# Attention front re-ordered: x in halves, rows of four heads sent out first, second batch split by ScalarE and GpSimd, first turn of the maxima earlier and on two queues

## Chip, cores and metric

One core of a Trainium2 chip runs the whole program. The metric is device time of one execution in microseconds (us); lower is better. Engines: TensorE (PE), VectorE (DVE), ScalarE (ACT), GpSimd (POOL), and SyncE (SP), which only issues transfers here. "SPq" and "ACTq" in the rows are transfers issued by SP and ACT.

## What is computed

Two layers of a small network on x of 2 batches x 1024 tokens x 128 channels. Only the first block matters for the change:

```python
mod = (silu(L0_c) @ L0_wmod)          # sa, ca, ga, sb, cb, gb: six rows of 128 for each batch
h = layernorm(x) * (1 + ca) + sa
q, k, v = h @ Wq.T, h @ Wk.T, h @ Wv.T     # 16 heads of 8 channels
attn = softmax(q @ k.T / sqrt(8))          # 1024 x 1024 for each of 2 x 16 heads
x = x + ga * (attn @ v)
```

Behind it follow a coupling network, two Mamba blocks and a mixture of 8 experts, which the change doesn't touch.

## The kernel before

Everything is written out by hand: each engine has its own instruction stream, in program order, and semaphores tie them together (`wait_ge`, `then_inc`). An engine whose next instruction waits does nothing else.

**Exact products from bfloat16.** The products q.k need float32 precision, so every q and k value is split into three bfloat16 parts: `hi` = the value rounded, `mid` = the rounded rest, `lo` = the rest of the rest. `pe_project` (L774) makes a float32 chunk of q or k (128 rows, which are 16 heads x 8, by 512 tokens) in a PSUM bank. ACT copies it to bfloat16 (`ac_part_hi`, L780), DVE subtracts (`part_rest`, L787) and, for the first batch, casts to `mid` (L791). For the second batch ACT casts (`ac_part_mid`, L796). GpSimd makes `lo` (L801). A side (0 = q, 1 = k) and a chunk c (0, 1 = first batch, 2, 3 = second) name a tile; `project(c)` does both sides.

**Way through DRAM.** SP writes the parts to the DRAM tensor `qk_parts` (`sp_parts_out`, L804, six transfers of 128 partitions for a batch, 256 KB each). They come back stacked in 48 rows for a head (`q_rows`, `k_rows`), so that one bfloat16 matmul of 48 rows sums all part products. The first group is heads 0 to 3: `load_first` (L518) brings heads 0 and 2 (12 transfers of 8 rows, on SP and ACT), `sp_load(0, 1)` heads 1 and 3. GpSimd's `po_ones` (L476) sets rows of ones in `k_rows`.

**Maxima ahead.** The softmax needs each query's maximum before its exponentials. The 32 heads are done in 16 legs (`NLEG`) of 4 heads x 512 queries. A leg has 16 tiles of maxima: two matmuls into `max_ps` (L559, `pe_max_score`) and one DVE reduction of 128x1024 (L570, `ve_max_score`); two such tiles fit in PSUM, so the matmuls of tile t wait for the reduction of tile t-2. `AHEAD` = 22 tiles are done before the main loop, by `ahead(v)` for v = 0 to 21. When a leg's 16 tiles are done, GpSimd splits the maxima (L579 to L585), PE turns them (`pe_max_turn`, L601), ACT copies the turned rows (L607), and SP writes them under the `q_rows` in four transfers (`sp_max_turn`, L610), so that the second pass of scores (L678) comes out with the maximum taken off. The main loop (L932) then weaves maxima (m), scores and exponentials (s, ACT, L686) and products with v (v, L706); its first item is one half of maxima tile 22, its second is the first score.

**Order of the front, before.** Layer norm of the first batch: 8 statistics, 8 `bn_aggr`, one GpSimd root of 128x8 (`ln_root`, L362), 8 `ve_ln_apply` (L358). Then transposes (`turn`, L398; L409 on PE, L416 on ACT), `project(0)`, `project(1)`, `values` (v, L814), parts out, the rows of layer 0's modulation (`mod_row`, L296, a matmul and an ACT copy each), the loads of the first group, layer norm and transposes of the second batch, the rows and columns of layer 1's modulation, and only then `ahead(0)`, `project(2)`, `ahead(1)`, `ahead(2)`, `project(3)`, `values(2)`, `values(3)`, parts out, `ahead(3)` to `ahead(21)`. The turn of leg 0 stands in `ahead(18)`:

```python
if v == NU + 2:
    ...
    max_turn(0)
    for half in range(2):
        sp_load(1, half)
```

The four PSUM banks of `score_k` are handed round as a ring (`ring.take`): `turn`, `pe_project`, `values`, `mod_row` and `pe_mod_cols` each take the next bank and wait until ACT or DVE has read what was in it.

## Time and profile before

| | us |
|---|---|
| median of 3 runs | 1132.33 (1130.43 to 1132.64) |
| the profiled execution's own time | 1135.81 |
| its span | 1134.5 |
| first tile of maxima starts on PE | 30.73 |
| first score of the main loop on PE | 60.94 |

Busy shares over the span: PE 92%, DVE 85%, ACT 72%, GpSimd 46%. Those are means over stages with different limits; the change lies in the first 61 us. The times in the rows are us from the span's start, save where ns is said. A float32 matmul appears as two records, and the ends of matmuls are modelled; starts are to be trusted more. "idle before" names how long the engine had nothing and what released it.

### The profile page before, as it was taken

Reading aid. Unit: us, or ns where it says so; the run is one execution under the profiler, and the core shown is the slowest. Engines: PE = TensorE matmul, PEld = TensorE weight load, DVE = VectorE, ACT = ScalarE, POOL = GpSimd, SP = SyncE. Lnnn points to the kernel's source line nnn. Section 1 sums busy time; section 2 is a strip of 40 time slices with the busy share of each in tenths; the row PEclk is TensorE's granted clock in tenths of the full one; section 3 lists DMA queues with packets and bytes.
Section 4 is the critical chain, followed back from the end, with each engine's and each line's share of the span. In section 5 each row is a group of like instructions: output and inputs, shape, how many; then the busy total and the mean of one; then the engine's idle time right before and its main releaser. Section 6 shows DMA issues by size and latency. Waiting matters only on the chain. (4 is left out here: it accounts for less than half of the span.)

```text
span 1134.5 us, 21410 instructions
## 1 busy us (share of the span) xinstructions
PE 1043.9 (92%) x7835; PEld 650.8 (57%) x7835; DVE 969.5 (85%) x1327; ACT 818.4 (72%) x1593; POOL 517.9 (46%) x487
## 2 busy tenths in 40 slices
PE   6899999999999887989999999899999996599997
PEld 4222222222222333458988984468888984388896
DVE  6899999999995676979999996989999999866666
ACT  3279898999999544978888854888888833246652
POOL 5400441010101111027889982048999974146663
PEclk9779999999999888799999999899999997699999
DMA  5210100001004420107999980118999977512224
GB/s 158 71 44 15 30 16 17 29 16 31 16 2 76 131 57 2 59 1 191 241 249 226 221 210 3 59 28 191 232 246 230 229 184 259 131 50 64 62 64 126
DMA packets 60313, 121.04 MB, mean 107 GB/s; under 512 B 15471, under 2 KB 28783, under 8 KB 59953
## 3 DMA queue, kind: packets, MB, share of 16 engines
q0 software_dynamic: 15440, 52.66, 23.2%
q1 hardware_dynamic: 43064, 64.82, 18.6%
q10 hardware_dynamic: 1704, 2.20, 0.6%
q8 instruction: 63, 1.03, 0.4%
q14 instruction: 42, 0.34, 0.1%
HBM read 58.02 MB, written 13.19 MB: 63 GB/s over the span
## 5 line engine op out<-in xcount | busy, mean ns | idle before, releaser
L2267 PEld LDWEIGHTS m_pair<-filter_w,delta_x_t 128*128 128x128 f32 x2560 | 294.0, 192 | 43.3 <-issue 43.3
L2267 PE MATMUL m_pair<-filter_w,delta_x_t 128*128 128x112 f32 (+3 forms) x2560 | 298.7, 276 | 9.4 <-DVE h_t L2294 4.1
L570 DVE TENSOR_REDUCE neg_max<-max_ps 128x1 f32<-128x1024 f32 x256 | 293.5, 1214 | 10.8 <-PE max_ps L559 10.5
L686 ACT ACTIVATE exp_scores<-score_k 128x512 f32<-128x512 f32 x512 | 273.9, 599 | 20.7 <-PE score_k L678 13.4
L2243 ACT ACTIVATE decay<-delta,a_log 128x1024 f32<-128x1024 f32 x128 | 145.7, 1142 | 50.0 <-DVE normed L2294 28.7
L559 PE MATMUL max_ps<-k_rows,q_rows 48*128 48x512 bf16 x512 | 166.8, 404 | 7.7 <-DVE neg_max L570 6.5
L2235 ACT ACTIVATE filter_w<-filter,b_t 128x112 f32<-128x112 f32 (+1 forms) x576 | 167.4, 374 | 0.0
L706 PE MATMUL score_k<-exp_scores,v_cols 128*32 128x256 f32 x2048 | 165.1, 396 | 0.0
L678 PE MATMUL score_k<-q_rows,k_rows 51*128 51x512 bf16 x512 | 162.8, 391 | 0.6 <-DMA q_rows<-neg_max_rows 0.6
L579 POOL CAST neg_max_parts<-neg_max 128x16 bf16<-128x16 f32 x16 | 3.1, 196 | 228.8 <-DVE neg_max L570 228.8
L559 PEld LDWEIGHTS max_ps<-k_rows,q_rows 48*128 48x128 bf16 x512 | 30.1, 95 | 120.6 <-DVE neg_max L570 91.9
L706 PEld LDWEIGHTS score_k<-exp_scores,v_cols 128*32 128x32 f32 x2048 | 40.9, 108 | 98.9 <-ACT exp_scores L686 80.1
L2285 DVE TENSOR_TENSOR_SCAN m_pair<-decay,m_pair 128x1024 f32<-128x1024 f32 x38 | 87.0, 2290 | 1.6 <-PE m_pair L2267 1.2
L2332 POOL TENSOR_TENSOR h_t<-h_t,c_row 128x1024 f32<-128x1024 f32 x30 | 81.5, 2717 | 13.1 <-DVE h_t L2294 13.1
L2332 POOL TENSOR_TENSOR normed<-normed,c_row 128x1024 f32<-128x1024 f32 x28 | 75.8, 2706 | 24.1 <-DVE normed L2294 24.1
L2294 DVE TENSOR_TENSOR_SCAN normed<-decay,m_pair 128x1024 f32<-128x1024 f32 x32 | 73.0, 2281 | 8.7 <-PE m_pair L2267 8.7
L2294 DVE TENSOR_TENSOR_SCAN h_t<-decay,m_pair 128x1024 f32<-128x1024 f32 x32 | 73.0, 2281 | 6.0 <-PE m_pair L2267 6.0
L2380 PE MATMUL m_pair<-delta_x,ident 128*128 128x512 f32 x136 | 68.3, 598 | 0.0
L2962 ACT ACTIVATE silu_gate<-gate 128x512 f32<-128x512 f32 x39 | 24.5, 628 | 55.4 <-DVE gate L2957 50.9
L2989 POOL DMA_INDIRECT moe_out_rows<-tile_out,row_to x37 | 39.8, 1075 | 42.1 <-DVE tile_out L2983 34.7
L2919 POOL DMA_INDIRECT tile_rows<-moe_normed,row_from x39 | 37.9, 972 | 37.5 <-DVE row_to L2794 25.9
L2935 ACT ACTIVATE gate_up<-gate_up_all 128x1024 f32 x39 | 41.1, 1056 | 17.8 <-DVE row_empty L2792 17.1
(343 smaller groups left out, 1726.9 us busy)
## 6 DMA issues: line engine op xcount, KB each, us to landing
c_row<-c_rows SPq DMA_DIRECT2D x64, 512.0 KB, 6.3
x_inner<-normed POOLq DMA_DIRECT2D x16, 512.0 KB, 6.7
delta_x<-mod_memory POOLq DMA_DIRECT2D x15, 512.0 KB, 8.0
delta_x<-x_inner POOLq DMA_DIRECT2D x15, 512.0 KB, 9.0
x_inner<-h_t POOLq DMA_DIRECT2D x14, 512.0 KB, 6.5
mod_memory<-h_t POOLq DMA_DIRECT2D x14, 512.0 KB, 9.1
mod_memory<-normed POOLq DMA_DIRECT2D x12, 512.0 KB, 9.3
gate_up_all<-in_gate_up_w SPq DMA_DIRECT2D x8, 512.0 KB, 7.5
```

Of the source, the lines that this page charges most:

```text
L559: mm = pe.matmul(mps[:, t % 2 * 2 + half, :], qp[row:row + KR, s, leg % 2, qt * P:(qt + 1) * P], kp[row:row + KR, s, half * CH:(half + 1) ...
L570: ve.tensor_reduce(nm[leg % 2][:, 4 * j + qt:4 * j + qt + 1], mps[:, bank:bank + 2, :].rearrange("p a q -> p (a q)"), AX_X, ALU.max, negat ...
L678: pe.matmul(eps[:, bank, :], kp[row:row + KM, s, kt * P:(kt + 1) * P], qp[row:row + KM, s, leg % 2, :], start=True, stop=True).then_inc(*s ...
L686: ac.activation(pt[a % 4][:, HEADS[r % 4], :], eps[:, bank, :], ACT.Exp, scale=SC).then_inc(*exped.up())
L706: mm = pe.matmul(eps[32 * j:32 * j + 32, av_bank[leg], qs], va[quad % 2][:, j, kt, :], pt[a % 4][:, j, qs], start=(kt == half == 0), stop= ...
L2235: w = ac.activation(wf[g % 3][:, lo:c * STEP + P], tri[min(c, 1)][:], ACT.Copy, scale=self.bT[b][:, c, n:n + 1])
L2243: ac.activation(da[u % 4], delta[:, blk, b, :], ACT.Exp, scale=am[:, l, blk, n:n + 1]).then_inc(*decay.up())
L2267: mm = pe.matmul(vps[blk][:, lo:hi], self.duT[b][:, c, blk * P:(blk + 1) * P], wf[g % 3][:, lo:hi], start=True, stop=True)
L2285: ve.tensor_tensor_scan(to, da[u % 4], vps[0][:], 0.0, ALU.mult, ALU.add).then_inc(*hs.up())
L2294: ve.tensor_tensor_scan(hh[g % 4], da[u % 4], vps[1][:], 0.0, ALU.mult, ALU.add).then_inc(*hs.up())
L2332: po.tensor_tensor(yacc[b][1] if n == 1 else hh[g % 4], hh[g % 4], csb[g % 3][:], ALU.mult).then_inc(*yg.up())
L2380: pe.matmul(yps[:, c * CH:(c + 1) * CH], self.ident[:], yp[k][:, c * CH:(c + 1) * CH], start=False, stop=last, skip_group_check=True).then ...
```

## The change

- x of the first batch comes in two transfers of four tiles each, and each half has statistics, aggregation and a root of its own; x of the second batch is issued behind six weight transfers. The load of layer 1's modulation moves on ACT's queue behind `silu` and `identb`. `silu` of layer 1 and its spread move behind the first group's loads. `ve_mod_cols(0)` moves behind the first batch's `ve_ln_apply`.
- The first batch's four tiles: `mid` is cast by DVE for tile 0 alone and by ACT for the other three; `lo` is GpSimd's for tiles 0 to 2 and DVE's for tile 3.
- The parts of heads 0 to 3 (32 of 128 partitions) go out first; those of heads 4 to 15 are issued behind the first group's loads. In `load_first`, ACT issues q's `hi` alone (3 transfers); SP issues the other nine.
- `po_ones(2, NS)` moves ahead of the second batch's work on GpSimd.
- The second batch: ACT makes `hi` and also copies the float32 values to SBUF, GpSimd subtracts (`rest`), ACT casts `mid`, GpSimd makes `lo`. DVE has no part in it. One tile stands behind each of `ahead(0)` to `ahead(3)`, `values` behind `ahead(4)` and `ahead(5)`, a `mod_row` of layer 1 behind each of `ahead(6)` to `ahead(9)`, the matmuls of its columns behind `ahead(10)` and their reading behind `ahead(12)`. Both transposed chunks of the second batch are read by ACT.
- The turn of leg 0 moves from `ahead(18)` to `ahead(17)`, its four transfers are issued two by SP and two by ACT, and the second batch's parts go out behind `ahead(21)`, so behind the 18 transfers of `sp_load(1, ...)`.

```diff
-            def sp_max_turn(leg):
-                sp.wait_ge(turn_read.sem, leg + 1)
-                for j in range(4):
-                    s, row = head_rows(leg, j)
-                    sp.dma_start(qp[row + KR:row + KM, s, leg % 2, :].rearrange("a (k q) -> a k q", k=4),
-                                 mt[leg % 2][12 * j:12 * j + 12, :]).then_inc(*max_in[leg % 2].up(16))
+            def put_max_turn(leg):
+                for engine, heads in ((sp, (1, 0)), (ac, (3, 2))) if leg == 0 else ((sp, range(4)),):
+                    engine.wait_ge(turn_read.sem, leg + 1)
+                    for j in heads:
+                        ...
...
+            self.ac_load_modulation(1)
+            half = TB // 2
+            roots = [self.ln_root(self.X, i * half, (i + 1) * half, [self.in_x[i].at()]) for i in range(2)]
+            self.po_spread(0)
+            normed = [self.ve_ln_apply(self.X, t, roots[t // half]) for t in range(TB)]
+            self.ve_mod_cols(0, cols_ps)
+            scaled = self.m_scale
+            root = self.ln_root(self.X, TB, NT, [self.in_x[2].at()])
...
-                if v == NU + 2:
+                if v == NU + 1:
                     for m in ring.out():
                         pe.wait_ge(*m)
+                    pe.wait_ge(*self.identb_set.at())
                     max_turn(0)
+                    for part in range(3):
+                        sp.wait_ge(*to_dram[0][part].at())
+                    sp.wait_ge(*rows_set.at())
                     for half in range(2):
                         sp_load(1, half)
...
+                def first_batch_parts():
+                    tiles, rest_in = [(c, side) for c in range(2) for side in range(2)], []
+                    for n, tile in enumerate(tiles):
+                        bank = ring.take()
+                        pe_project(*tile, bank)
+                        ac_part_hi(*tile, bank)
+                        rest_in.append(ve_part_rest(*tile, bank))
+                        if n == 0:
+                            po_part_lo(*tile, ve_part_mid(*tile, rest_in[0]))
+                        if n > 1:
+                            po_part_lo(*tiles[n - 1], ac_part_mid(*tiles[n - 1], rest_in[n - 1]))
+                    ve_part_lo(*tiles[3], ac_part_mid(*tiles[3], rest_in[3]))
...
+                def second_batch_parts(c, side):
+                    bank = ring.take()
+                    pe_project(c, side, bank)
+                    ac_part_hi(c, side, bank)
+                    ac_part_copy(c, side, bank)
+                    rest_in = po_part_rest(c, side, bank)
+                    if rest_known:
+                        second_batch_mid()
+                    rest_known.append(((c, side), rest_in))
...
-                for c in range(2):
-                    project(c)
+                first_batch_parts()
                 for c in range(2):
                     values(c)
-                sp_parts_out(0)
-                rows_in[0] = [self.mod_row(0, j) for j in range(4)]
+                sp_parts_out(0, range(4), ((part_hi.at(),), (part_mid.at(), part_ve.at()), (part_po.at(), part_ve.at())))
                 for engine in (sp, ac):
                     engine.wait_ge(*early_rows)
+                first_q = qp[:].rearrange("d s a q -> d s (a q)")
                 for part in range(3):
                     load_first(sp, kp, 1, part)
-                    load_first(ac if part < 2 else sp, qp[:].rearrange("d s a q -> d s (a q)"), 0, part)
+                    load_first(sp if part else ac, first_q, 0, part)
                 sp_load(0, 1)
-                po.wait_ge(*part_lo.at())
+                sp_parts_out(0, range(4, H), ((), (), ()))
+                self.ac_silu_c(1)
+                rows_in[0] = [self.mod_row(0, j) for j in range(4)]
+                self.po_spread(1)
                 po_value_columns()
+                po_ones(2, NS)
                 ve.wait_ge(*self.ln_aggr.at())
                 normed += [self.ve_ln_apply(self.X, t, root) for t in range(TB, NT)]
-                self.turn(normed, col(1), col(0), (scaled,), done=ht, by=(0, 0, 0, 1), chunks=(2, 3))
-                rows_in[1] = [self.mod_row(1, j) for j in range(4)]
-                self.ve_mod_cols(1, self.pe_mod_cols(1))
-                ahead(0)
-                project(2)
-                ahead(1)
-                ahead(2)
-                project(3)
-                for c in range(2, NC):
-                    values(c)
-                sp_parts_out(1)
-                po.wait_ge(*part_lo.at())
-                po_ones(2, NS)
-                sp.wait_ge(*rows_set.at())
+                self.turn(normed, col(1), col(0), (scaled,), done=ht, by=(0, 0, 0, 0), chunks=(2, 3))
+                for v in range(AHEAD):
+                    ahead(v)
+                    if v < 4:
+                        second_batch_parts(2 + v // 2, v % 2)
+                    elif v < 6:
+                        if rest_known:
+                            second_batch_mid()
+                        values(v - 2)
+                    elif v < 10:
+                        rows_in[1].append(self.mod_row(1, v - 6))
+                    elif v == 10:
+                        cols_ps = self.pe_mod_cols(1)
+                    elif v == 12:
+                        self.ve_mod_cols(1, cols_ps)
+                sp_parts_out(1, range(H), ((part_hi.at(),), (part_mid.at(),), (part_po.at(),)))
...
-            pe.wait_ge(*self.identb_set.at())
-            for v in range(3, AHEAD):
-                ahead(v)
```

## Rows read from the trace of the kernel before

**Rows 1.** Page, part 5, the two costliest groups of the attention loop.

```profile
L570 DVE TENSOR_REDUCE neg_max<-max_ps 128x1 f32<-128x1024 f32 x256 | 293.5, 1214 | 10.8 <-PE max_ps L559 10.5
L686 ACT ACTIVATE exp_scores<-score_k 128x512 f32<-128x512 f32 x512 | 273.9, 599 | 20.7 <-PE score_k L678 13.4
```

**Rows 2.** Windows: each engine's busy time (instructions), granted clock, DMA share, GB/s.

```profile
23.50:24.00 0.50, 0.00 (x0) 0.00 (x0) 0.50 (x2) 0.00 (x0) 0.50 (x1) 1.00 0.95 295
25.00:25.50 0.50, 0.50 (x4) 0.38 (x3) 0.25 (x1) 0.00 (x0) 0.00 (x0) 0.50 0.88 295
28.00:28.50 0.50, 0.50 (x2) 0.24 (x2) 0.00 (x0) 0.32 (x2) 0.00 (x0) 0.93 0.23 78
...
81.00:102.00 21.00, 21.00 (x225) 5.82 (x223) 20.53 (x20) 20.26 (x40) 1.95 (x9) 1.00 0.11 33
```

**Rows 3.** Timeline of DVE, 0 to 70 us: start, length, what.

```profile
5.07 1.65 DVE L346 BATCH_NORM_STATS2 bn_parts<-x 128x6 f32<-128x128 f32 x8 [5.07 <-DMA x<-in_L_attn_x]
...
15.21 0.69 DVE L787 TENSOR_TENSOR part_rest<-score_k,part 128x512 f32<-128x512 f32 x1 [0.93 <-ACT part L782]
15.94 0.43 DVE L791 CAST part<-part_rest 128x512 bf16<-128x512 f32 x1
...
17.00 0.88 DVE L791 CAST part<-part_rest 128x512 bf16<-128x512 f32 x1
...
20.84 4.42 DVE L358 TENSOR_SCALAR normed<-x,mean_var,rstd 128x128 f32<-128x128 f32 x8
...
31.37 1.23 DVE L570 TENSOR_REDUCE neg_max<-max_ps 128x1 f32<-128x1024 f32 x1
...
38.48 22.40 DVE L570 TENSOR_REDUCE neg_max<-max_ps 128x1 f32<-128x1024 f32 x19 [0.42 <-PE max_ps L559]
```

**Rows 4.** Timeline of PE, 0 to 70 us.

```profile
12.50 4.62 PE L777 MATMUL score_k<-h_t,w_qkv 128*128 128x512 f32 x8
16.95 1.95 PE L814 MATMUL score_k<-w_qkv,h_t 128*128 128x128 f32 x16
...
24.22 1.56 PE L409 MATMUL score_k<-ident,normed 128*128 128x128 f32 x6 [1.57 <-DVE normed L358]
...
29.40 1.40 PE L256 MATMUL score_k<-silu_c,mod_memory 128*128 128x2 f32 x12
30.73 0.60 PE L559 MATMUL max_ps<-k_rows,q_rows 48*128 48x512 bf16 x2
31.26 1.98 PE L777 MATMUL score_k<-h_t,w_qkv 128*128 128x512 f32 x4
...
56.00 0.30 PE L601 MATMUL score_k<-identb,neg_max_parts 128*48 128x128 bf16 x1
...
60.94 0.61 PE L678 MATMUL score_k<-q_rows,k_rows 51*128 51x512 bf16 x1 [0.59 <-DMA q_rows<-neg_max_rows]
```

**Rows 5.** Timeline of GpSimd, 0 to 70 us.

```profile
22.24 1.85 POOL L750 MEMSET v_cols<- 128x1024 f32 x2
...
38.20 2.27 POOL L801 TENSOR_TENSOR part<-part_rest,part 128x512 bf16<-128x512 f32 x2 [1.39 <-ACT part L796]
40.52 7.06 POOL L478 MEMSET k_rows<- 32x4096 bf16 x2
```

**Rows 6.** Groups by shape: busy us, mean ns | idle before.

```profile
L342 POOL TENSOR_TENSOR rstd<-var_eps,minus_half 128x4 f32<-128x4 f32 x2 | 2.0, 1010 | 0.2
```

**Rows 7.** Timeline of ACT, 0 to 70 us.

```profile
14.58 0.60 ACT L782 ACTIVATE part<-score_k 128x512 bf16<-128x512 f32 x1 [1.12 <-PE score_k L777]
...
56.34 0.27 ACT L607 ACTIVATE neg_max_rows<-score_k 48x128 bf16<-48x128 bf16 x1 [16.27 <-PE score_k L601]
```

**Rows 8.** Timeline of SP: the transfers that it issues.

```profile
17.78 0.58 SPq L808 DMA_DIRECT2D qk_parts<-part  x1
...
27.59 0.31 SPq L523 DMA_DIRECT2D q_rows<-qk_parts  x1
...
56.68 3.15 SPq L614 DMA_DIRECT2D q_rows<-neg_max_rows  x4
```

**Rows 9.** The issues of `sp_parts_out` (L808) by line: time to landing.

```profile
DMA to landing us min/median/max: 2.8/2.9/4.3
```

More of the change, by code:

```diff
@@ L193, in constants @@
         self.gtmp = {n: sb(f"gate_tmp{n}", [P, 2 * n]) for n in (NB, NB * D)}
-        self.in_x = [self.sig(f"in_x{b}") for b in range(NB)]
+        self.in_x = [self.sig(n) for n in ("in_x_first", "in_x_next", "in_x_second_batch")]
         self.in_c = [self.sig(f"in_c{l}") for l in range(2)]
@@ L207, in constants @@
         self.ac_load_modulation(0)
-        for b in range(NB):
-            sp.dma_start(self.X[:, b * TB:(b + 1) * TB, :],
-                         A["L0_attn_x"][b].rearrange("(k p) d -> p k d", p=P)).then_inc(*self.in_x[b].up(16))
-            if b == 0:
-                sp.dma_start(self.ident[:], A["k_ident"]).then_inc(*self.in_k.up(16))
+        for half in range(2):
+            lo = half * TB // 2
+            sp.dma_start(self.X[:, lo:lo + TB // 2, :], A["L0_attn_x"][0][lo * P:(lo + TB // 2) * P].rearrange(
+                "(k p) d -> p k d", p=P)).then_inc(*self.in_x[half].up(16))
+        sp.dma_start(self.ident[:], A["k_ident"]).then_inc(*self.in_k.up(16))
         po.memset(self.half[:], -0.5).then_inc(*self.const_set.up())
@@ L782, in ac_part_hi, with ve_part_rest @@
                     ac.activation(p[0][:, side, c * CH:(c + 1) * CH], bank.ps[:], ACT.Copy).then_inc(*part_hi.up())
-                def ve_part_mid(c, side, bank):
+                def ve_part_rest(c, side, bank):
                     cs = slice(c * CH, (c + 1) * CH)
@@ L825, in ac_values, with second_batch_mid @@
                     return bank.left
-                def project(c):
-                    banks = [ring.take() for _ in range(2)]
-                    for side in range(2):
-                        pe_project(c, side, banks[side])
-                        ac_part_hi(c, side, banks[side])
-                        ve_part_mid(c, side, banks[side])
-                        if c < 2:
-                            po_part_lo(c, side)
-                    if c > 1:
-                        for side in range(2):
-                            ac_part_mid(c, side, banks[side].left)
-                            po_part_lo(c, side)
+                def first_batch_parts():
[10 more added lines that the diff above has]
+                    ve_part_lo(*tiles[3], ac_part_mid(*tiles[3], rest_in[3]))
+                rest_known = []
+                def second_batch_mid():
+                    tile, rest_in = rest_known.pop()
+                    po_part_lo(*tile, ac_part_mid(*tile, rest_in))
+                def second_batch_parts(c, side):
[7 more added lines that the diff above has]
+                    rest_known.append(((c, side), rest_in))
                 def values(c):
```

77 lines of the change are left out of this document (45 added, 32 removed).

## The prediction

> **What bounds the kernel now.** I read the page first, then the timelines of the five engines from 0 to 70 us, then windows of half a microsecond for the clock. In the attention loop all three large engines are nearly full: in 21 us PE shows 21.00, DVE 20.53, ACT 20.26 [rows 2]; its costliest groups, 256 reductions and 512 exponentials, hardly idle [rows 1]. The change alters nothing there, for the same 22 tiles are ahead. So what counts is when the first score starts, 60.94 us [rows 4], and everything behind it should move with it.
>
> What sets 60.94? Go backwards. The score waited 0.59 us for the turned maxima's rows [rows 4]. Their four transfers were issued from 56.68 for 3.15 us [rows 8], behind ACT's copy at 56.34 [rows 7] and the turn at 56.00 [rows 4]. Had they been in, the score would still have stood behind the first half of maxima tile 22, which waits for the reduction of tile 20. The reductions are a stream: tile 0 starts at 31.37, the last 19 run without a gap from 38.48 to 60.88, 1.18 us each [rows 3]. 22 of them need 25.9 us; the stream took 60.88 - 31.37 = 29.5. The missing 3.6 us are the second batch's four subtractions, 4 x 0.69 = 2.8, and gaps of 0.8 around them [rows 3]. And why does tile 0 start so late? PE came to its matmuls at 30.73, straight from layer 1's columns (29.40, 1.40 us long), so PE's order had the last word there [rows 4]. The data weren't much earlier: SP's last issue for the first heads was at 27.59 [rows 8], and landing takes some 1.7 us, which I estimate from the turned rows (last of four issues begun near 59.1, score released at 60.94 [rows 4, 8]). That gives 29.3.
>
> **The change, part by part.** I follow the new order with these durations.
>
> *Layer norm.* x lands at 5.07 as a whole [rows 3]; its first half can't take longer, and I take 4.2. Four statistics (0.21 each) and four aggregates lead to a root of 1.01 for 4 columns [rows 3, 6], so both halves are normalized by about 9.3. But the scale comes from PE's columns, whose inputs the change hardly hastens, so I let the first projection start near 11.3, against 12.50 [rows 4].
>
> *First batch's parts.* The first projection took 2.08 us from start to ACT (12.50 to 14.58 [rows 4, 7]), PE being slow there; two at full speed took 1.98 with their modelled end [rows 4], 0.86 apart. So `hi` of the four tiles is ready at 17.3 (ACT now has a cast in between), against 17.78, when SP saw it before [rows 8]. The casts and `lo` end at 19.4: one DVE cast less per tile removes 0.43 to 0.88 each [rows 3], and DVE does the last `lo` (0.69, priced as the subtraction L787) beside GpSimd's 1.14 [rows 5]. Before, SP could issue `lo` at about 22.3, since 6 issues of about 0.6 end where its loads begin.
>
> The row shows a DVE cast of 0.43 alone and 0.88 beside GpSimd's `lo`, and eight normalizations of 4.42 in all while GpSimd set `v_cols` from 22.24 [rows 3, 5]. The Trainium skill ("SBUF — State Buffer", Who interferes with whom) says that such a DVE instruction and a GpSimd one exclude each other for a whole instruction, and that a DVE instruction with two SBUF inputs waits for a GpSimd one that reads. By that rule DVE's last `lo` would wait for GpSimd's, 0.5 us later than I have it; by it, too, reductions never wait for GpSimd. The trace agrees on the latter: the 19 reductions keep 1.18 beside 7.06 us of GpSimd's fills [rows 3, 5].
>
> *Out and back.* SP issues `hi` at 17.3, `mid` at 19.4 (its mark is DVE's count after the last `lo`), `lo` at 20.5. Unknown is what a transfer of 32 partitions costs: an issue between 0.31 (8 rows) and 0.58 (128 rows) [rows 8], landing between 2.8 and 4.3 [rows 9]. I take 0.55 and 2.9, the short end, for a quarter of the bytes. `lo` is in at 23.9. SP's nine loads (2 more than before) take about 0.4 each and the last is issued near 25.0, in at 26.8. With landing 4.3 it is 28.2; with everything short, 25.3. ACT's q loads and the layer 0 rows are done by 25, the second batch's transposes by 26, so PE waits for the data: **tile 0 at 26.8 instead of 30.73, 3.9 sooner**. The normalizations have 1 to 2 us of cover there; if GpSimd's fills of 3.5 us each (half of 7.06 [rows 5]) caught one, it would be gone.
>
> *The stream of maxima.* From a first reduction at 27.4, 22 x 1.175 = 25.9 us would end at 53.3. DVE gets `ve_mod_cols(1)`, 0.45. The four subtractions are gone from it (ACT 0.60 each for the copy, GpSimd about 1.2 each, nearest `lo` 1.14 [rows 5]; 1.4 at most would add 1 us to its chain). But PE now has work between the tiles. At full clock: 12 pairs x 0.43, four projections x 0.86, two `values` (1.95 for two [rows 4]), four rows (2 x 0.86 + 2 x 0.43), columns 1.40: 14.6 us until tile 11. The clock will not be full all the time. Before, PE was empty for 1.57 us until 24.22 [rows 4], and the granted clock was 0.50 by 25.0, 0.93 at 28.0 again [rows 2]; after, PE is sparse from 20 to 26.8. I charge 4 us at half speed, so 2 us: 16.6. DVE alone would reach tile 11 after 11 x 1.175 + 0.6 = 13.5. The difference, **3.1 us, is stalls of DVE behind PE**.
>
> *Behind them the banks.* GpSimd's `po_ones` (7.06) and `v_cols` (1.85 and two short ones) [rows 5] now precede its subtractions. They start when ACT has done layer 1's `silu`, about 22.2, and end near 31.8. ACT's `mid` of the first tile waits for the first subtraction (33.0), and behind it in ACT's order stand `hi` and copy of tile 2, and so on; ACT frees `values(2)`'s bank near 40.3, `mod_row`'s third take needs it, and PE comes there at 39.4. This adds 0.9. `max_turn(0)`'s copy comes near 51, 9 us after ACT's last of these, so it isn't touched. Nor are the second batch's parts: leg 4 is their first user.
>
> *The turn.* One tile earlier and two queues: PE comes to the turn 1.18 earlier than the 56.00 of before, 1.0 after tile 15's reduction (60.88 - 6 x 1.18 = 53.8), about when GpSimd's split is done; with 0.6 for turn and copy [rows 4, 7] and the hand-over the copy ends 1.75 after that reduction, two issues on each side take 3.15 / 2 = 1.6 [rows 8], landing 1.8: 5.1 after tile 15. PE reaches the score after tile 20's reduction (5 x 1.175 = 5.9) and 0.43 for the first half of tile 22. The wait is gone and the score starts 0.7 before the last reduction ahead ends, where before it started with its end: 0.7 to 0.8 won. ACT's two issues lie before a table load and the first exponential; both fit in.
>
> **Sum.** Last reduction ahead: 27.4 + 25.9 + 0.45 + 3.1 + 0.8 = 57.6. First score 56.9, against 60.94: **4.0 us sooner**. In terms: start -3.9, subtractions and gaps -3.6, columns +0.45, stalls +3.1, banks +0.8, turn -0.75. The profiled execution took 1135.81, so it would be 1131.8; the median of the runs is 3.5 below it: 1132.33 - 4.0 = **1128.3 us**. The loop's start at half clock stays as it was: PE is again sparse for over 10 us before it.
>
> **Rivals.**
> - *Transfers are better than priced and PE's clock holds.* Tile 0 at 25.3 (1.5 more), the 2 us at half speed and part of the bank wait fall away, too: 6.5 won, 1125.8. For it: a quarter of the bytes. Against: PE's idle stretch. Chance 0.19.
> - *Transfers are the bound and don't shrink.* Landing 4.3 for each part and nine issues on one queue: tile 0 at 28.5 to 29, about 2 won, 1130.3. For it: before, `lo` needed the long landing. Chance 0.19, split by the 0.2% bound.
> - *A start gained and lost again later*: the loop's start moves against the clock's dips, or ACT and PE run slower through the first exponentials. Loss 2 to 4 us, 1131 to 1133, no change. Against: loads and weights further back have no absolute due time. Chance 0.11.
> - *Slower: the clock stays at half through the interleaving.* PE's 14.6 us become about 29, less what DVE hides; tile 11's matmuls end near 56 instead of 44, and the score starts 8 us later than before: 1140. It decides from stalls of 3.1 + 4.8 = 7.9 us, that is, from roughly 8 us at half clock instead of 4. For it: a projection behind each pair doubles PE's need just when its clock is low. Against: in the same front, the clock was back 4 us after dense work began at 24.22 [rows 2, 4]. Chance 0.08.
>
> My forecast gets 0.43. 0.2% is 2.3 us, about what a measurement of this kernel tells from no change; the bound is 1130.07. Faster: 0.43, 0.19, and half of the second rival, 0.09, together 0.71. Same: 0.10 of the second and 0.10 of the third, 0.20. Slower: 0.08 and 0.01 of the third, 0.09. The range reaches from the first rival with a microsecond more to the third: 1124.3 to 1132.3; it leaves out the fourth and the far ends.
>
> **What would show it.** `part` out at 17.3 and again for the other heads behind the loads; the first `max_ps` matmul at 26.8 with a DMA as its releaser; no `part_rest` on DVE beyond 20; DVE gaps with PE as releaser among the first 12 reductions, 3 to 4 us in all; the first score near 56.9 with no wait on a DMA. A first tile later than 29, or gaps above 8 us, makes the prediction wrong; so does a score on time with an end that isn't.

## The result and the profile after

| | before | after |
|---|---|---|
| median of six runs each, us | 1132.34 (1130.43 to 1135.05) | 1148.11 (1146.29 to 1152.20) |
| profiled execution: own time / span, us | 1135.81 / 1134.5 | 1149.29 / 1148.0 |
| mean granted clock of TensorE | 0.941 | 0.931 |

The change is slower: the ratio is 1.0144, with an interval from 1.0121 to 1.0167. I had predicted 1128.3 and put 1140 at a chance of 0.08. The medians differ by 15.8 us, the two profiled executions by 13.5; the account below is that of the profiled ones.

The page of the kernel after, the group of the reductions. It answers to the first of [rows 1]: the reductions take as long as before, but DVE stands idle in front of them, behind PE, for 36.4 us instead of 10.5.

```profile
L571 DVE TENSOR_REDUCE neg_max<-max_ps 128x1 f32<-128x1024 f32 x256 | 294.1, 1211 | 36.5 <-PE max_ps L560 36.4
```

The timeline of DVE after:

```profile
18.73 1.00 DVE L826 TENSOR_TENSOR part<-part_rest,part 128x512 bf16<-128x512 f32 x1 [0.70 <-ACT part L814]
...
28.89 1.22 DVE L571 TENSOR_REDUCE neg_max<-max_ps 128x1 f32<-128x1024 f32 x1 [7.11 <-PE max_ps L560]
31.85 1.22 DVE L571 TENSOR_REDUCE neg_max<-max_ps 128x1 f32<-128x1024 f32 x1 [1.74 <-PE max_ps L560]
...
60.46 2.35 DVE L571 TENSOR_REDUCE neg_max<-max_ps 128x1 f32<-128x1024 f32 x2 [2.39 <-PE max_ps L560]
...
69.19 5.93 DVE L571 TENSOR_REDUCE neg_max<-max_ps 128x1 f32<-128x1024 f32 x5 [0.20 <-PE max_ps L560]
```

This is where the time went. The stream of maxima starts earlier (28.89 against 31.37 in [rows 3]), and then its first eleven tiles take 60.46 - 28.89 = 31.6 us where DVE alone needs 11 x 1.175 = 12.9: **18.6 us of stalls**, 1.74 between most neighbours, all with a PE matmul as releaser. PE's own timeline says why:

```profile
11.43 5.09 PE L780 MATMUL score_k<-h_t,w_qkv 128*128 128x512 f32 x8 [0.78 <-ACT h_t L418]
...
23.28 1.07 PE L411 MATMUL score_k<-ident,normed 128*128 128x128 f32 x8 [2.25 <-issue]
27.82 1.03 PE L560 MATMUL max_ps<-k_rows,q_rows 48*128 48x512 bf16 x2 [3.47 <-DMA q_rows<-qk_parts]
28.78 2.07 PE L780 MATMUL score_k<-h_t,w_qkv 128*128 128x512 f32 x2
30.79 1.03 PE L560 MATMUL max_ps<-k_rows,q_rows 48*128 48x512 bf16 x2
...
72.82 0.60 PE L680 MATMUL score_k<-q_rows,k_rows 51*128 51x512 bf16 x1
```

A pair of maxima takes 1.03 with its modelled end, against 0.60 in [rows 4]. There is no gap between the entries from 27.82 on: PE works all the time, slowly. The windows show the clock (columns: us, length, busy us of PE, weight loads, DVE, ACT, GpSimd with instructions, granted clock, DMA share, GB/s):

```profile
20.00:22.00 2.00, 1.03 (x4) 0.38 (x2) 1.78 (x7) 0.04 (x1) 0.00 (x0) 1.00 0.18 57
...
24.00:26.00 2.00, 0.35 (x4) 0.11 (x2) 0.00 (x0) 1.55 (x3) 1.89 (x5) 0.63 0.37 115
26.00:28.00 2.00, 0.18 (x1) 0.12 (x2) 0.00 (x0) 0.00 (x0) 2.00 (x1) 0.50 0.45 124
...
27.50:61.00 33.50, 33.18 (x70) 12.00 (x70) 14.00 (x12) 9.97 (x24) 13.82 (x10) 0.50 0.15 46
...
73.00:86.00 13.00, 12.44 (x68) 1.86 (x64) 10.49 (x9) 8.69 (x16) 0.00 (x0) 0.50 0.52 165
86.00:107.00 21.00, 21.00 (x225) 5.84 (x221) 20.16 (x18) 20.14 (x39) 0.83 (x4) 1.00 0.07 20
```

The clock falls from 1.00 to 0.50 (from 2.4 to 1.2 GHz) near 24.5: the 0.63 is the mean of 24 to 26. PE's wait for the first rows has then only just begun; ahead of it lie the transposes of 1.07 us and a standstill of 2.25. The clock stays at half for over 60 us, although PE is busy for 33.18 us of the 33.50 from 27.5 to 61. It is back at 86. So the first score starts at 72.82, against 60.94, and the loop's first 13 us run at half clock.

The kernel before loses the clock at the same time, as its windows show (stretches that [rows 2] hasn't), but is back at 28, behind transposes and rows of layer 1. What it has and the kernel after hasn't is the rise, not a clock that never falls. Its loop runs at half clock for 8 us:

```profile
24.50:25.00 0.50, 0.50 (x4) 0.35 (x2) 0.50 (x3) 0.00 (x0) 0.00 (x0) 0.65 0.94 295
...
61.00:69.00 8.00, 7.62 (x39) 1.29 (x39) 6.61 (x6) 6.31 (x12) 0.00 (x0) 0.50 0.32 97
```

ACT's first exponential comes 11.9 us later than before, its copy at the end of the loop's first leg 14.35 later (99.55 against 85.20), the copy of the last leg 14.05 later (383.66 against 369.61), the end of the span 13.5 later. From the first leg's copy to the last's both kernels take nearly the same time, 284.4 us before and 284.1 after, with 18.77 us for most legs. So the loss arises ahead of 100 us.

The following three views serve the account of the single terms below. SP's timeline:

```profile
17.33 5.03 SPq L835 DMA_DIRECT2D qk_parts<-part  x6
...
25.91 0.30 SPq L524 DMA_DIRECT2D q_rows<-qk_parts  x1
...
68.52 1.54 SPq L616 DMA_DIRECT2D q_rows<-neg_max_rows  x2
```

Time to landing of the issues of L835, all 18 of them (before: [rows 9]):

```profile
DMA to landing us min/median/max: 2.9/3.4/3.9
```

ACT's timeline:

```profile
68.22 0.27 ACT L608 ACTIVATE neg_max_rows<-score_k 48x128 bf16<-48x128 bf16 x1 [11.96 <-PE score_k L602]
68.52 1.63 ACTq L616 DMA_DIRECT2D q_rows<-neg_max_rows  x2
...
73.47 1.73 ACT L688 ACTIVATE exp_scores<-score_k 128x512 f32<-128x512 f32 x3 [2.00 <-PE score_k L680]
```

### The profile page after: what moved, and what is told of

The parts are those of the page before. It is cut to its first block and busy times, and to the rows that moved or that the text cites. A ratio compares the mean times of both kernels' runs of the same rounds, so it can differ in the third digit from the quotient of the medians.

```text
span 1148.0 us, 21428 instructions
## 1 busy us (share of the span) xinstructions
PE 1054.6 (92%) x7835; PEld 655.2 (57%) x7835; DVE 966.8 (84%) x1320; ACT 821.5 (72%) x1601; POOL 522.4 (46%) x492
## 3 DMA queue, kind: packets, MB, share of 16 engines
q8 instruction: 63, 1.03, 0.4%
## 5 line engine op out<-in xcount | busy, mean ns | idle before, releaser
L571 DVE TENSOR_REDUCE neg_max<-max_ps 128x1 f32<-128x1024 f32 x256 | 294.1, 1211 | 36.5 <-PE max_ps L560 36.4
L560 PE MATMUL max_ps<-k_rows,q_rows 48*128 48x512 bf16 x512 | 170.3, 411 | 9.2 <-DVE neg_max L571 5.2
L2377 POOL TENSOR_TENSOR normed<-normed,c_row 128x1024 f32<-128x1024 f32 x28 | 76.4, 2727 | 23.7 <-DVE normed L2339 23.7
L2377 POOL TENSOR_TENSOR h_t<-h_t,c_row 128x1024 f32<-128x1024 f32 x30 | 81.4, 2714 | 11.9 <-DVE h_t L2339 11.8
L3007 ACT ACTIVATE silu_gate<-gate 128x512 f32<-128x512 f32 x39 | 24.5, 628 | 55.7 <-DVE gate L3002 44.7
L2980 ACT ACTIVATE gate_up<-gate_up_all 128x1024 f32 x39 | 41.1, 1056 | 17.9 <-DVE row_empty L2837 17.1
```

Of the source, the lines that this page charges most:

```text
L560: mm = pe.matmul(mps[:, t % 2 * 2 + half, :], qp[row:row + KR, s, leg % 2, qt * P:(qt + 1) * P], kp[row:row + KR, s, half * CH:(half + 1) ...
L571: ve.tensor_reduce(nm[leg % 2][:, 4 * j + qt:4 * j + qt + 1], mps[:, bank:bank + 2, :].rearrange("p a q -> p (a q)"), AX_X, ALU.max, negat ...
L2377: po.tensor_tensor(yacc[b][1] if n == 1 else hh[g % 4], hh[g % 4], csb[g % 3][:], ALU.mult).then_inc(*yg.up())
```

## The experiments

Theory A: PE's wait in front of tile 0 lets the clock fall, and the work that is woven between the tiles doesn't bring it back. Rivals: the woven order itself costs this much at any clock (B); GpSimd's and ACT's longer chain for the second batch holds the banks (C); the transfers or their small pieces (D). Every kernel computes the full result; the matmuls that some of them add are extra work whose result nobody reads. The times are medians, each beside that of the kernel before on the same chip; since those differ (1118 to 1132), only ratios are compared between chips. A ratio with an interval is the recorded estimate, which needn't be the quotient of the two medians; a kernel that ran once has no interval. What is said of clocks and of times within the kernel comes from one trace of each.

### Fill PE's wait, with full rows and with fewer (e1_fill, e2_fill48)

```diff
+                def pe_fill(n, rows=P):
+                    for _ in range(n):
+                        pe.matmul(mps[:, 3, :], w[0:rows, 0, :], self.HT[0:rows, 0:CH], start=True, stop=True)
...
                 rows_in[0] = [self.mod_row(0, j) for j in range(4)]
+                pe_fill(2)
...
                 self.turn(normed, col(1), col(0), (scaled,), done=ht, by=(0, 0, 0, 0), chunks=(2, 3))
+                pe_fill(4)
                 for v in range(AHEAD):
```

The second kernel has `pe_fill(2, 48)` and `pe_fill(4, 48)`: the same matmuls with 48 of the 128 rows.

> The changed kernel with six float32 matmuls of 128 rows x 512 columns added on TensorE, whose results nobody reads: two behind the rows of layer 0 and four between the transposes of the second batch and the first tile of maxima, where TensorE was idle. Theory A (the clock: TensorE's idle stretch before the first tile lets the granted clock fall to half, and the woven work between the tiles then runs at half): the clock stays 1.00 through the interleaving, tiles 0 to 10 come 1.5 to 2 us apart instead of 3.0, the first score starts at 56 to 59 us instead of 72.8, and the time is 1128 to 1133. Rival B (weaving other matmuls between the tiles costs this much at any clock): first score still beyond 68 us, time 1144 or more. Rival C (the clock is low for another reason than idleness, such as the kind of work): clock 0.50 again by 35 us, time over 1142.

> As the fill with 128 rows, but the six added matmuls use 48 of the 128 rows, for the same time. If any busy time holds the clock, this gives the same as the full fill: clock 1.00, 1128 to 1133. If the number of rows in use counts, the clock falls as without a fill: 0.50 from about 26 us on, first score near 73, time near 1148.

With full rows 1118.96 against 1118.81, ratio 1.0006 (0.9990 to 1.0022). Its windows and DVE's timeline:

```profile
24.00:28.00 4.00, 3.89 (x16) 2.27 (x16) 0.00 (x0) 2.60 (x6) 3.88 (x6) 1.00 0.37 117
...
32.00:46.00 14.00, 14.00 (x59) 5.99 (x58) 11.38 (x10) 8.53 (x22) 10.32 (x9) 1.00 0.26 85
```

```profile
31.32 1.23 DVE L571 TENSOR_REDUCE neg_max<-max_ps 128x1 f32<-128x1024 f32 x1 [0.37 <-PE max_ps L560]
...
46.80 2.36 DVE L571 TENSOR_REDUCE neg_max<-max_ps 128x1 f32<-128x1024 f32 x2 [0.74 <-PE max_ps L560]
```

With 48 rows a single run gave 1133.46, ratio 1.013, as slow as the change. Its windows and PE's timeline:

```profile
24.00:28.00 4.00, 4.00 (x15) 1.88 (x13) 0.00 (x0) 1.90 (x4) 3.88 (x5) 1.00 0.40 127
28.00:32.00 4.00, 4.00 (x8) 1.11 (x8) 1.58 (x2) 1.09 (x2) 3.94 (x2) 0.61 0.37 111
32.00:46.00 14.00, 14.00 (x32) 5.23 (x31) 5.77 (x5) 6.63 (x17) 9.73 (x9) 0.50 0.22 74
```

```profile
28.17 0.59 PE L560 MATMUL max_ps<-k_rows,q_rows 48*128 48x512 bf16 x2
28.69 1.96 PE L780 MATMUL score_k<-h_t,w_qkv 128*128 128x512 f32 x2
30.58 1.03 PE L560 MATMUL max_ps<-k_rows,q_rows 48*128 48x512 bf16 x2
```

The first run takes the whole loss away with nothing but filler, so the clock is the cause, and B, C and D can at most hold the rest. The second is finer than theory A: there PE never waits (4.00 of 4.00 from 24 to 32), the pair of tile 0 still runs at the full clock, and within a microsecond the clock goes down. In this run a busy PE wasn't enough; what it worked on counted. And the woven order, the same in both, keeps the full clock where it meets it (1.00 from 32 to 46) and the half where it meets that. Two groups from tile 0 to tile 12 (windows from 28 to 61 and from 29 to 47), first the kernel after, then e1_fill (busy us, mean ns | idle):

```profile
L560 PE MATMUL max_ps<-k_rows,q_rows 48*128 48x512 bf16 x26 | 13.2, 619 | 3.5 <-DMA q_rows<-qk_parts 3.5
L780 PE MATMUL score_k<-h_t,w_qkv 128*128 128x512 f32 x8 | 8.3, 1141 | 0.0
```

```profile
L560 PE MATMUL max_ps<-k_rows,q_rows 48*128 48x512 bf16 x26 | 7.7, 381 | 0.3 <-DMA q_rows<-qk_parts 0.3
L780 PE MATMUL score_k<-h_t,w_qkv 128*128 128x512 f32 x8 | 4.5, 644 | 0.0
```

The same instructions in the same number take 13.2 instead of 7.7 us and 8.3 instead of 4.5. And even at the full clock the first eleven tiles take 46.80 - 29.73 = 17.1 us, 4.1 more than DVE alone: a pair and one woven item (a projection or a part of the values) are 1.59, and DVE's reduction of 1.23 is done 0.37 earlier.

### Layer 1's rows and columns ahead of the tiles again (e3_rows_first), and the woven order alone (e4_before_spread)

```diff
                 self.turn(normed, col(1), col(0), (scaled,), done=ht, by=(0, 0, 0, 0), chunks=(2, 3))
+                rows_in[1] = [self.mod_row(1, j) for j in range(4)]
+                self.ve_mod_cols(1, self.pe_mod_cols(1))
                 for v in range(AHEAD):
...
-                    elif v < 10:
-                        rows_in[1].append(self.mod_row(1, v - 6))
-                    elif v == 10:
-                        cols_ps = self.pe_mod_cols(1)
-                    elif v == 12:
-                        self.ve_mod_cols(1, cols_ps)
```

The other kernel is the one before, with these lines moved the other way, and projections and values one behind each tile; ACT and DVE split as before.

> The changed kernel with the rows and columns of layer 1's modulation back in front of the first tile of maxima, where they stood before the change. They fill TensorE's idle stretch with work that has to be done. Theory A: the first tile starts 1 to 2 us later (29 to 30 us), but the clock is 1.00 by 30 us, 4 to 5 us of work are gone from between the tiles, first score 56 to 60 us, time 1128 to 1134. Rival B: only the removed work is saved, at half clock 9.9 us of it less 2 us of later start: first score near 65, time near 1140. Rival C: as B.

> The kernel before with only its order behind the transposes changed as in the changed kernel: one tile of the second batch behind each of the first four tiles of maxima, then values, rows and columns one by one; all else (transfers, VectorE's subtractions, the turn) as before. Theory A: TensorE reaches the first tile from sparse work, waits for data, the clock is half and stays there; first score at 68 to 74 us, time 1140 to 1148: the loss comes from this part alone. If it comes from other parts (ScalarE's copy, GpSimd's subtractions, transfers), the time is within 3 us of 1132.

e3: 1117.82 against 1118.81, ratio 0.9992 (0.9978 to 1.0007). e4, one run: 1134.94, ratio 1.014. Windows of e3, and its timelines of DVE and ACT:

```profile
24.00:28.00 4.00, 3.78 (x20) 2.75 (x20) 0.00 (x0) 3.79 (x10) 3.88 (x6) 1.00 0.38 115
...
46.00:60.00 14.00, 12.05 (x32) 1.66 (x31) 13.80 (x13) 3.68 (x6) 1.54 (x8) 0.50 0.15 43
58.00:70.00 12.00, 11.44 (x64) 1.86 (x64) 9.74 (x9) 8.52 (x16) 0.00 (x0) 0.50 0.57 173
```

```profile
39.33 14.02 DVE L571 TENSOR_REDUCE neg_max<-max_ps 128x1 f32<-128x1024 f32 x12 [0.40 <-PE max_ps L560]
```

```profile
57.83 4.57 ACT L688 ACTIVATE exp_scores<-score_k 128x512 f32<-128x512 f32 x8 [2.00 <-PE score_k L680]
```

And e4's PE:

```profile
29.75 1.03 PE L559 MATMUL max_ps<-k_rows,q_rows 48*128 48x512 bf16 x2 [4.06 <-DMA q_rows<-qk_parts]
30.72 2.07 PE L777 MATMUL score_k<-h_t,w_qkv 128*128 128x512 f32 x2
32.72 1.03 PE L559 MATMUL max_ps<-k_rows,q_rows 48*128 48x512 bf16 x2
```

In e4 nothing else of the change is in, and the whole loss is there: a wait of 4.06 us, tiles 2.97 apart, first exponential at 76.4. In e3 all else is in, and the loss is gone. So one part of the change did it: the 5 us of layer 1's rows and columns used to fill the wait for the transfers, with matmuls on all 128 rows, and were moved behind it. In e3 PE also stands for 2.22 us in front of the transposes, as in the change, but dense work follows from 24.22 to tile 0 and the clock stays at 1.00.

e3 is nearly the front that I had predicted: first exponential at 57.8 instead of 61.6, 3.8 sooner. But the end doesn't show it. At the end of the first leg 1.3 us of it are left (83.94 against 85.20), at the last leg 1.7 (367.93 against 369.61). The windows say where it went: the clock, which fell at 44 when only tiles of 48 rows were left for PE, stays at half until 70, for 13 us of the loop instead of 8.

### Keep the clock up behind tile 6 (e5_warm, e6_before_warm, e9_warm192, e10_warm256)

```diff
+                def pe_warm(rows=P, cols=384):
+                    pe.wait_ge(ring.free[7], ring.used[7])
+                    pe.matmul(eps[:, 3, 0:cols], w[0:rows, 0, :], self.HT[0:rows, 0:cols], start=True, stop=True)
...
                         values(v - 2)
+                    if v >= 6:
+                        pe_warm()
```

This stands on e3 (384, 192 and 256 columns), and for e6 on the kernel before, behind each of the tiles 3 to 21.

> The kernel with the rows and columns of layer 1 in front, and one float32 matmul of 128 rows x 384 columns added behind each of the tiles of maxima 6 to 21, whose result nobody reads. The kernel without them started its exponentials 3.75 us sooner than the kernel before, but its clock came back only at 70 us, after 12 us of loop at half clock (before: 7.5 us), and the whole was 1 us faster. Theory A (the lead is given back because the sparse stretch grew in front of the loop and the loop runs slowly at half clock): the clock stays 1.00 from 30 us into the loop, the first exponential comes at 57 to 58 us, tile 30 starts at 66 to 67.5 us instead of 70.7, and the time is 3 to 5 us below the kernel without, 0.3 to 0.4% below the kernel before. Rival D (the loop's start is limited by ScalarE and the products with v, not by the clock, or the lead is lost further back): no faster than 0.9992 of before. Rival E: the added matmuls hold up the tiles, which VectorE should finish 1.18 us apart: tiles over 1.25 us apart, time the same or worse.

> The kernel before with the same added matmuls behind tiles 3 to 21. Theory A: its clock stays 1.00 from 42 to 68 us as well, and its 7.5 us of loop at half clock go: 1.5 to 2.5 us faster, 0.15 to 0.2%. Rival D: no change. If it gains as much as the front with the rows first does by these matmuls, the new front is worth nothing of its own.

> The kernel with the rows of layer 1 in front and a float32 matmul of 128 rows x 192 columns behind tiles 6 to 21 (384 columns held the clock at 1.00 up to the loop, but put the tiles 1.375 us apart and the first exponential at 61.4 instead of 57.8; the last exponential came at 365.6, as without them). By theory A a smaller fill leaves VectorE its 1.18 us; if it still holds the clock: tiles 1.18 to 1.22 apart, first exponential 57.5 to 58.5, last exponential at 362 to 363 us, 3 to 4 us ahead of the kernel without, time 0.9965 to 0.998 of before. If the smaller share doesn't hold the clock: 0.50 from about 45 us, last exponential at 366, time as without.

> The same with 256 columns: clock 1.00 up to the loop more likely, tiles 1.20 to 1.28 apart, last exponential at 362 to 364 us.

| kernel | time / before | ratio (interval) | clock | first exponential |
|---|---|---|---|---|
| e5_warm | 1117.48 / 1118.23 | 1.0007 (0.9984 to 1.0030) | full from 20 | 61.4 |
| e6_before_warm | 1121.01 / 1118.23 | 1.0013 (0.9991 to 1.0035) | full from 30 | 64.8 |
| e9_warm192 | 1132.31 / 1131.48 | 1.0007 (0.9987 to 1.0027) | 1.00 until some 54, then half until 68 | 59.8 |
| e10_warm256 (one run) | 1130.89 / 1131.48 | not measured | half from 62 to 68 | 58.3 |

DVE in e5:

```profile
42.17 1.23 DVE L571 TENSOR_REDUCE neg_max<-max_ps 128x1 f32<-128x1024 f32 x1 [0.15 <-PE max_ps L560]
```

With 384 columns the clock holds, and the loop's first leg takes 22.3 us from the first exponential, against 23.6 before and 26.1 in e3. But each tile pays: PE is now 1.375 a tile and DVE waits 0.15 behind it. The filler costs what the clock gives, and the 3 to 5 us that I had expected didn't come. 256 columns are the size that DVE hides (tiles 1.175 apart), but then the clock still falls once the loop has begun.

### The other parts one by one (e7_turn_old, e8_out_whole, e12_vector_rest)

The turn of before on e3; the change with all sixteen heads' parts sent out at once; and e3 with the subtractions of the second batch on DVE again.

```diff
e7  -                if v == NU + 1:
    +                if v == NU + 2:
    -                for engine, heads in ((sp, (1, 0)), (ac, (3, 2))) if leg == 0 else ((sp, range(4)),):
    +                for engine, heads in ((sp, range(4)),):
e8  -                sp_parts_out(0, range(4), (...))
    +                sp_parts_out(0, range(H), (...))
    -                sp_parts_out(0, range(4, H), ((), (), ()))
e12 -                    ac_part_copy(c, side, bank)
    -                    rest_in = po_part_rest(c, side, bank)
    +                    rest_in = ve_part_rest(c, side, bank)
```

> The kernel with the rows and columns of layer 1 in front, but the turn of leg 0 in the place of before (behind tile 18) and its four transfers all on SP's queue. By the prediction the first score then waits for the rows again, some 0.6 to 0.8 us: first exponential near 58.6 instead of 57.83, time 0 to 1 us longer, not to be told from noise.

> The changed kernel, but the parts of all 16 heads go out in one piece ahead of the first group's loads, 128 partitions at a time as before. By the prediction a quarter of the bytes lands earlier: the first tile of maxima, which waits for it at 27.8 us in the changed kernel, then comes 1 to 3 us later, and PE's idle stretch grows as much; the time 1 to 3 us longer, at the unchanged half clock. If the size of the pieces doesn't count: first tile at 27.8 within 0.4.

> The kernel with the rows of layer 1 in front, but the second batch's subtractions back on VectorE (one of 0.69 us behind each of tiles 0 to 3) in place of ScalarE's copy and GpSimd's subtraction. In the kernel without this VectorE idles 0.36 us behind each of these tiles, since TensorE is the limit there. So each tile grows by 0.3 to 0.7 us: first exponential 1.2 to 2.8 us later than 57.8, last exponential as much later or less. If the subtractions were free in their old place: first exponential at 57.8 to 58.2.

e7: 1117.13 against 1118.23, ratio 0.9988 (0.9966 to 1.0011), first exponential at 59.0, 1.2 later than e3; 0.4 of that is a later tile 0. The turn is worth about 0.8 at its place and nothing that the end shows. e8, one run: 1133.38 (1.013), tile 0 at 28.12 instead of 27.82. I had expected 1 to 3 us. Even these 0.3 can't be told from nothing: e11 below is the change up to tile 0, and starts it at 28.66. So the small pieces neither won the time that I had priced nor caused the loss, and D falls. e12, one run: 1129.7 against 1131.48. DVE's timeline shows each of the four subtractions between two of the first reductions; this is the first of them:

```profile
31.54 0.69 DVE L790 TENSOR_TENSOR part_rest<-score_k,part 128x512 f32<-128x512 f32 x1 [0.46 <-ACT part L785]
32.15 1.22 DVE L571 TENSOR_REDUCE neg_max<-max_ps 128x1 f32<-128x1024 f32 x1
```

Its first exponential is at 58.1, e3's at 57.8, and their last legs end at 367.91 and 367.93. Here I had expected 1.2 to 2.8 us and missed. In the woven order DVE waits 0.37 a tile for PE anyway (e1). A subtraction puts the reduction behind it off by 0.6, so it fills this wait and the first tiles are 1.73 apart instead of 1.59, which is made up where DVE would have waited for the values: moving the subtractions to ACT and GpSimd gained 0.3 us at most. C falls as well, for e4 has the old split and the whole loss.

### Dense work behind tile 0 (e11_late_fill)

```diff
                     ahead(v)
+                    if v == 0:
+                        pe_fill(5)
```

> The changed kernel with five float32 matmuls of 128 rows x 512 columns added behind the first tile of maxima, so after the clock has fallen. At half clock they cost up to 8.6 us. If dense 128-row work is what raises the clock (theory A, from the rise at 28 us in the kernel before): 1.00 by 33 us, tiles then 1.6 us apart instead of 3.0, first exponential at 62 to 65 us instead of 73.5, time 8 to 11 us below the changed kernel's. If the clock stays at 0.50 whatever is run (a limit of another kind): first exponential beyond 78 us, 5 to 8 us slower than the changed kernel.

One run: 1138.50 against 1131.48, ratio 1.006. Windows, and PE's timeline:

```profile
28.00:32.00 4.00, 3.34 (x5) 1.30 (x6) 1.23 (x1) 0.00 (x0) 3.94 (x2) 0.50 0.41 115
32.00:34.00 2.00, 2.00 (x4) 0.72 (x3) 0.00 (x0) 0.00 (x0) 1.08 (x1) 0.72 0.65 222
34.00:38.00 4.00, 4.00 (x11) 1.36 (x9) 0.66 (x1) 1.08 (x2) 0.00 (x0) 1.00 0.44 151
```

```profile
29.62 6.29 PE L890 MATMUL max_ps<-h_t,w_qkv 128*128 128x512 f32 x10
```

Here the wait and the half clock at tile 0 are as in the change (the fall comes at 26.3, later than there), and 6.29 us of unread matmuls make it faster than the change by more than half the loss: the clock is back at 33, and the tiles that follow are 1.59 apart. It is the plainest proof that the woven order, not the wait alone, kept the clock down.

### A version with both fills (e13_warm_loop, e14_before_warm_loop, e15_guarded)

```diff
                 wait_from(pe, *free)
+                if leg == 0 and r < 10 and r % 2 == 0:
+                    pe.matmul(eps[:, bank, 0:256], w[:, 0, :], self.HT[:, 0:256], start=True, stop=True)
                 pe.matmul(eps[:, bank, :], kp[row:row + KM, s, kt * P:(kt + 1) * P], qp[row:row + KM, s, leg % 2, :],
```

e13 is e3 with 256 columns behind the tiles 6 to 21 and this in the loop; e14 has both on the kernel before; e15 is e13 with `pe_fill(2)` behind layer 0's rows and `pe_fill(1)` in front of tile 0.

> The kernel with the rows of layer 1 in front, a float32 matmul of 128 rows x 256 columns behind tiles 6 to 21, and one more of these ahead of every second of the first ten scores, into the bank that the score then overwrites. If the half clock at the loop's start takes the lead back: clock 1.00 throughout, first exponential at 58 to 59 us, last exponential at 361.5 to 363.5 us instead of 366, time 0.9960 to 0.9980 of before. If not: last exponential at 365.5 or later, ratio 0.999 or more.

> The kernel before with the same fills (tiles 3 to 21 and the first scores). Its first exponential stays near 61.6 to 62; with a full clock its last exponential comes 2 to 3 us sooner than 367.6, at 364.5 to 365.5 us, time 0.9975 to 0.9995 of before. The difference of the two, 2.5 to 3.5 us, is then what the new front is worth by itself.

> The kernel with the rows of layer 1 in front and fills of 256 columns up to the first scores, and three more float32 matmuls of 128 rows x 512 columns: two behind the rows of layer 0, where TensorE idles near 22 us, one in front of the first tile of maxima. Theory A: no run falls to half clock for long (no run over 1145 us), clock 1.00 from 20 to 75 us, first exponential at 58 to 60 us, last exponential at 362 to 364, time 0.9965 to 0.9985 of before. If the fall isn't due to idleness: again some runs 30 us above the others.

| kernel | time / before | ratio (interval) |
|---|---|---|
| e13_warm_loop | 1129.37 / 1131.53 | 0.9974 (0.9953 to 0.9994) |
| e14_before_warm_loop | 1130.97 / 1131.53 | 0.9995 (0.9979 to 1.0012) |
| e15_guarded | 1130.55 / 1131.80 | 0.9979 (0.9962 to 0.9997) |

On the kernel before the two fills win nothing: e14 has the full clock from 30 on, but its last leg ends at 369.82, against 369.61 without them, where I had expected 2 to 3 us.

Two of e13's 14 runs took 1160 us and are left out of its ratio; the profiled one is of these, and it shows how thin e3's cover is:

```profile
29.86 1.03 PE L560 MATMUL max_ps<-k_rows,q_rows 48*128 48x512 bf16 x2 [1.25 <-DMA q_rows<-qk_parts]
```

```profile
26.00:30.00 4.00, 2.75 (x18) 2.12 (x17) 0.58 (x3) 1.64 (x5) 3.94 (x2) 0.98 0.40 115
30.00:84.00 54.00, 54.00 (x107) 17.19 (x106) 26.93 (x22) 9.57 (x22) 13.40 (x17) 0.50 0.17 51
```

A wait of 1.25 us for a transfer, and the woven order and the tiles with their filler spend 54 busy us at half clock. e15 guards this place; none of its 12 runs was above 1132.1. That the guard is the reason is likely and not shown, with so few runs. In its profile the clock is 1.00 wherever I read it from 20 to 98, the loop's first leg ends at 83.66, the last at 367.59, 2.0 sooner than before. It beats the kernel before by 0.2%, at the edge of what can be told, and with it the changed kernel.

## Why the prediction was wrong

**The step that failed** is the sentence "I charge 4 us at half speed" in the stream of maxima, and with it the chance of 0.08 for the rival "the clock stays at half through the interleaving". The rival named the place, the point from which it decides (7.9 us of stalls) and a time of 1140; the stalls were 18.6. The half clock lasted 60 us, not 4. One sum of the rival is off: by the prediction's own price 7.9 us of stalls take 4.8 us more than 3.1, so 9.6 more at half clock and 13.6 in all, not 8. I had the evidence from [rows 2, 4]: the clock was back 4 us after dense work began. But that work was transposes, rows and columns on all 128 rows. I took it for any uninterrupted work, and the change weaves tiles of 48 rows with two float32 matmuls at a time. At the half clock that never raised it (after, e2, e4, e13); at the full clock it kept it (e1, e3). What lets the clock fall is less clear than that it didn't rise: it fell some 0.2 us into the wait in the change, some 1.2 into it in e11, which is the same kernel up to there, and in e2 with no wait at all in front of tile 0. Of the 18.6 us, 4.1 are the woven order at the full clock (e1) and 14.5 the clock.

A rule bears on each half. The Trainium skill ("TensorE: Matmul & The Clock Gate", HAM oscillation — how this bites in real kernels) has waits for transfers between bursts throttle PE: the trace agrees as far as the clock is at 0.50 behind the wait of 3.47 us, but it fell when some 0.2 us of it had passed, behind the standstill of 2.25. The Trainium skill's table of two states on the same page (Part 1, What's actually happening) gives the full clock to a PE that is continuously busy: here the trace differs, 33.18 of 33.50 us busy at 0.50, and the measurement decides.

**The other terms**, first score against 60.94. Start: -3.9 was -2.9. Projection (11.43, predicted 11.3) and first `hi` (17.33, predicted 17.3) were right. SP's six issues took 5.03 us, to 22.36, and transfers of this line landed after 2.9 to 3.9 us where I had put 2.9; so its last load went out at 25.91 instead of 25.0. Tile 0 followed 1.9 behind it, about the 1.8 that I had put, at 27.82 instead of 26.8 and within my bounds of 25.3 and 28.2. Subtractions and gaps, -3.6: they are gone from DVE, but e12 shows that this order gives 0.3 at most for it; the term was right as a sum and wrong as a gain, since it reappears as waiting for PE. Columns +0.45: right (0.16 and 0.24 at 62.7). Banks +0.8: nothing; GpSimd's 1.15 for a subtraction was right, but at 2.97 us a tile its chain had time to spare, and in e1 DVE's gaps name PE and hardly grow. Turn -0.75: right; the copy at 68.22, two issues on SP in 1.54 beside two on ACT in 1.63, and the score waits for no transfer; e7 gives 0.8. Sum: -2.9 - 3.6 + 0.45 + 18.6 - 0.75 = +11.8, measured +11.9.

**"The loop's start at half clock stays as it was"**, and "everything behind it should move with it", failed next. The time at which the clock comes back didn't move with the loop's start: after and e3 have 13 us of the loop at half, before 8. From first exponential to the end of the leg it is 26.1, 26.1 and 23.6 us, and 22.3 at the full clock (e5). So in its trace the change lost another 2.5 us there, and of e3's 3.8 only 1.3 to 1.7 reach the end. This is the third rival, a start gained and lost later; in e3's trace it came true, and its ratio of 0.9992 (0.9978 to 1.0007) can't tell the rest from nothing. But the loss isn't a price of the start alone. e7 differs from e3 only in the turn and starts its loop 1.2 later; it has the clock back at 68 and ends the leg sooner (83.43 against 83.94). e2 and e8 start theirs where the change does (72.6 and 73.1) and have it back near 83, not 86. What ends the half clock is not settled: PE is about 95% busy through those of before, after and e3.

**Layer norm and the last `lo`** were mis-sized by little. x's first half landed at 3.92 and its second at 6.01, where the whole had landed at 5.07 [rows 3]. The last `lo` on DVE took 1.00 instead of my 0.69 and began while GpSimd was at its own two (2.29 from 16.90): that lies between no delay and the 0.5 by the rule in the Trainium skill ("SBUF — State Buffer", Who interferes with whom), but no run shows what this instruction takes alone. It ended at 19.7 (predicted 19.4).

## What to carry to other kernels

Before moving work away from a wait, ask what that work does for the engine that waits: dense matmuls on all rows that "fill" PE also hold its clock, and may be worth more where they stand than in any gap behind. Price a stretch of PE work at the clock that it starts with, unless a row shows that this very mix of matmuls raised it; and check in which work the rise that you rely on took place. A start that comes sooner is worth what reaches the end of the next stage, which was a third to a half of it in e3.

## What the runs showed of the hardware

- The granted clock kept the state in which it met a mixed stretch: pairs of 48-row bf16 matmuls with pairs of float32 matmuls of 128 rows ran at 1.00 for 14 us fully busy (e1) and at 0.50 for over 33 us almost fully busy (after). With the filler of 256 columns behind the later tiles it was 0.50 for 54 us fully busy (e13).
- Filler on 48 rows kept PE busy for 4.00 of 4.00 us, and the clock fell just behind it, near 29, in the one run of e2; with the same filler on 128 rows it held (e1). Ten float32 passes on 128 rows in one go brought it back (e11).
- In the loop's first us a busy PE at half clock costs DVE and ACT too: from the first exponential to the end of the leg it is 23.6 to 26.1 us with 8 to 13 us at half (before, e3, after), and 22.3 at the full clock (e5).
- A transfer in two halves didn't deliver them both sooner (3.92 and 6.01 against 5.07), and parts of a quarter of the bytes brought no more than 0.3 us (27.82 against 28.12 in e8), less than the 0.84 by which after and e11 differ at the same place.
